# Two transformer layers on one core: another written order for the second layer's attention (jobs 60 ahead instead of 59)

## What is computed

```
x = x + attention_a(layernorm(x))      # 16 heads of 8, every query sees every key
x = x + ffn(layernorm(x))              # silu(x Wg) * (x Wu), then Wd; hidden 384
x = x + attention_b(layernorm(x))      # 16 heads of 8, causal: k_pos > q_pos is masked
x = x + ffn(layernorm(x))              # the same weights as the first ffn
```

## Time and profile before

| what | value |
|---|---|
| median of 3 runs | 1333.21 us (1331.5 to 1336.69) |
| the profiled execution | 1338.29 us, of which its span is 1336.4 us |
| PE busy | 1290.7 us, 97% of the span |
| DVE busy | 1176.7 us, 88% |
| ACT busy | 1004.5 us, 75% |
| first attention, full (from about 73 to 668 us) | 16 windows |
| causal attention, steady | from about 873 to 1222 us |

### The profile page before, as it was taken

One profiled execution on the slowest core, in us unless ns is written; L12 is line 12 of the kernel. 1 busy time (PEld: TensorE's weight loads), 2 busy tenths in 40 slices (PEclk: granted clock), 3 DMA queues, 4 the chain that ended last, 5 costly groups with the idle time before them and its releaser, 6 DMA issues.

```text
span 1336.4 us, 26857 instructions
## 1 busy us (share of the span) xinstructions
PE 1290.7 (97%) x9681; PEld 656.2 (49%) x9681; DVE 1176.7 (88%) x2979; ACT 1004.5 (75%) x1791; POOL 142.1 (11%) x309
## 2 busy tenths in 40 slices
PE   8899999999999999999988987999999999999998
PEld 6434343433434443434335764555555555555487
DVE  7699999999999999999926988799899999999276
ACT  8678888888888888888884531677777777777753
POOL 5630000000000000000002211200000000000011
PEclk9689999999999999999999996799999999999999
DMA  7611001111101111100000433112111211120001
GB/s 209 204 33 34 21 14 34 33 33 34 32 8 29 34 33 33 33 23 13 2 1 1 122 99 95 34 39 59 36 35 38 59 37 34 35 64 4 3 25 40
DMA packets 40060, 58.44 MB, mean 44 GB/s; under 512 B 7796, under 2 KB 19448, under 8 KB 39928
## 3 DMA queue, kind: packets, MB, share of 16 engines
q1 hardware_dynamic: 39928, 56.72, 17.7%
HBM read 36.77 MB, written 18.87 MB: 42 GB/s over the span
## 4 chain that ended last, share of the span: by engine, by line
PE 88%; DVE 5%; ACT 3%; issue 2%; DMA 1%; SPq 0%; POOL 0%; DVEq 0%; ACTq 0%; POOLq 0%
PE psum L1166 30%; PE psum L1132 21%; PE psum L1100 21%; PE psum L1253 4%; PE psum L1028 3%; PE psum L1237 2%; ACT probs L653 2%; PE psum L1140 2%; PE psum L1039 1%; DVE maxima L882 1%; DVE hid L958 1%; PE psum L1182 1%; PE psum L1077 1%; PE psum L1013 1%; PE psum L1150 1%
## 5 line engine op out<-in xcount | busy, mean ns | idle before, releaser
L653 ACT ACTIVATE probs<-psum 128x512 f32<-128x512 f32 (+3 forms) x1386 | 821.8, 669 | 153.0 <-PE psum L1132 83.0
L882 DVE TENSOR_REDUCE maxima<-psum 128x1 f32<-128x512 f32 x1232 | 767.8, 682 | 8.6 <-PE psum L1100 6.6
L1100 PE MATMUL psum<-kop,qop 62*128 62x512 f32 (+2 forms) x1744 | 519.4, 429 | 7.0 <-DVE maxima L879 3.1
L1132 PE MATMUL psum<-qop,kop 64*128 64x512 f32 (+3 forms) x1792 | 514.2, 427 | 9.2 <-ACT probs L653 7.9
L1166 PE MATMUL psum<-probs,v 128*32 128x512 f32 (+3 forms) x3584 | 440.5, 564 | 0.7 <-ACT sums L660 0.7
L1100 PEld LDWEIGHTS psum<-kop,qop 62*128 62x128 f32 x1744 | 266.4, 189 | 203.4 <-DVE maxima L882 119.3
L1132 PEld LDWEIGHTS psum<-qop,kop 64*128 64x128 f32 x1792 | 247.5, 187 | 232.1 <-ACT probs L653 205.9
L879 DVE CUSTOM_DVE_ANT_0 junk<-psum,mask 128x512 bf16<-128x512 f32 (+3 forms) x512 | 232.6, 487 | 38.7 <-PE psum L1100 34.9
L1166 PEld LDWEIGHTS psum<-probs,v 128*32 128x32 f32 x3584 | 71.1, 108 | 120.0 <-issue 89.2
L546 POOL TENSOR_TENSOR att<-att_raw,rden 128x128 f32<-128x128 f32 x64 | 26.1, 409 | 536.9 <-DVE rden L911 536.9
L1140 PE MATMUL psum<-half_ident,key_mask 64*128 64x64 bf16 x1024 | 74.3, 197 | 0.0
(11 more groups left out here) (102 smaller groups left out, 750.4 us busy)
## 6 DMA issues: line engine op xcount, KB each, us to landing
qop<-q_parts SPq DMA_DIRECT2D x256, 64.0 KB
kop<-k_parts SPq DMA_DIRECT2D x64, 128.0 KB
kop<-k_parts SPq DMA_DIRECT2D x128, 64.0 KB
q_parts<-parts SPq DMA_DIRECT2D x24, 256.0 KB, 2.9
k_parts<-parts SPq DMA_DIRECT2D x24, 256.0 KB, 3.2
x<-in_L_attn_a_x SPq DMA_DIRECT2D x8, 256.0 KB, 4.6
q_parts<-att SPq DMA_DIRECT2D x8, 256.0 KB, 3.7
k_parts<-att SPq DMA_DIRECT2D x8, 256.0 KB, 3.8
```

The source lines that it names most:

```text
L653: nc.scalar.activation(probs[:, slot, heads[0] % 2:heads[-1] % 2 + 1, c0:], psum[:, bank:bank + len(heads), c0:], ACT.Exp, scale=SCORE_SCA ...
L882: nc.vector.tensor_reduce(dst, src, AX_X, ALU.max).then_inc(ring_free, 1)
L1100: mm(psum[:, bank, 0:width], qop[rows, buf, f, r, qb * P:(qb + 1) * P].bitcast(F32R), kop[rows, buf, r, kh * CHUNK:kh * CHUNK + width].bit ...
L1132: ins = mm(psum[:, bank + k, c0:], kop[rows, buf, c // 2, j * P:(j + 1) * P].bitcast(F32R), qop[rows, buf, f, c // 2, c0:].bitcast(F32R), ...
```

## The change

One plan, that of the causal layer, gets another string, one more job ahead, and another order of the jobs within each half. Before, the turn of a window begins with two jobs, H, a job, a unit; the last sum of the window before (the first p) comes after three units (of steps 0, 0 and 1), and h, n, N stand together in the last quarter. After, the turn begins with two jobs and the owed sum, then H; n comes after two units and eight jobs of the new turn, and h and N stand together between the units of steps 6 and 7, without n. The numbers of letters are the same: 48 j, 24 s, 12 p and one each of H, h, N, n. `sums_behind` stays 1 and `project_at` stays (4, 6, 10).

```diff
          Plan(causal=True, heads=PAIR_UNITS, unit_ring=2, job_ring=3, alternate=True,
-              order="jjHjsjjsjjjspjssjjpjsjjsjspjjssjjpsjjpjssjjpjsjjsjpsjjjspjjssjjpjjsjspjjjhnNjjsjpjjssjjp",
-              jobs_ahead=59, sums_behind=1, project_at=(4, 6, 10),
-              tiles=("120 110 030 130 020 320 330 100 230 010 220 300 000 310 210 200",
...
+              order="jjpHjjsjjsjjnjjsjspjsjjspsjjspjsjsjjpsjjsjpsjjspjjhNjsjsjpjjssjjpjjsjsjjpjjssjjpjjsjsjp",
+              jobs_ahead=60, sums_behind=1, project_at=(4, 6, 10),
+              tiles=("200 010 230 330 000 130 320 020 100 030 110 120 310 210 300 220",
...
```

More of the change, by code:

```diff
@@ L156 @@
          Plan(causal=True, heads=PAIR_UNITS, unit_ring=2, job_ring=3, alternate=True,
-              order="jjHjsjjsjjjspjssjjpjsjjsjspjjssjjpsjjpjssjjpjsjjsjpsjjjspjjssjjpjjsjspjjjhnNjjsjpjjssjjp",
-              jobs_ahead=59, sums_behind=1, project_at=(4, 6, 10),
-              tiles=("120 110 030 130 020 320 330 100 230 010 220 300 000 310 210 200",
-                     "310 121 311 100 030 300 211 200 321 031 201 230 110 231 120 210 221 330 021 001 320 010 301 331 111 000 101 011 131 220 130 020"))]
+              order="jjpHjjsjjsjjnjjsjspjsjjspsjjspjsjsjjpsjjsjpjsjjspjjhNjsjsjpjjssjjpjjsjsjjpjjssjjpjjsjsjp",
+              jobs_ahead=60, sums_behind=1, project_at=(4, 6, 10),
+              tiles=("200 010 230 330 000 130 320 020 100 030 110 120 310 210 300 220",
+                     "301 030 311 021 031 320 011 101 000 310 330 231 201 110 100 210 010 131 111 130 220 121 020 120 230 331 221 211 300 200 321 001"))]
 SHIFT_PAIR = 2 * -(-[item[0] for item in PLANS[0].walk].index("shift") // 4)
```

## The result

The changed kernel took 1337.82 us (median of 20 runs, 1335.23 to 1342.44), the kernel before, run beside it, 1333.6 us (20 runs, 1331.5 to 1338.96). The ratio is 1.0026, with a 95% interval of 1.0015 to 1.0036: the change costs about 3.5 us. I had forecast 3.4 us gained.

A forecast was written before the change was run, and what follows sets the result against it. PE was taken as the bound, DVE close behind, ACT with room. Terms -3.2 - 0.5 + 0.3 = -3.4 us on 1333.21 gave 1329.8, forecast 1330; own range 1326 to 1332.5, 8-in-10 range 1322.5 to 1338.

The forecast's parts named there:

- ACT hides as before; cost 0, at worst 0.1 a period: Units of steps 4 to 8: PE has about 2.1 us for two units, ACT 75% busy, so no cost.
- The owed sum before H: Around H: two narrow sums let DVE catch up; PE's wait 0.58 becomes 0.35 us, 3.2 us gained over 14 periods.
- Rival 1: All waits go: none of the 0.58 us left, long periods normal, 9.1 gained, 0.3 lost, 1324.4 us; chance 0.18.
- n taken out of the bundle: Bundle h, n, N: no cost, at worst 0.2 us a period; three long periods shorten, 0.5 us gained, bounds 0 and 1.0.
- The end: Last turn, no jobs, ACT leads: n and N move ahead of the projection's start; 0, bounds 0.5 us either way.
- The start: Before window 0's first unit, 64 jobs instead of 62: net +0.3 us; clock unchanged, bounds 1.5 us either way.
- The sum: Whole kernel: -3.2 - 0.5 + 0.3 = -3.4 us, from the median 1333.21 to 1329.8, forecast as 1330.
- Rival 3: DVE becomes the bound in the nine jobs behind H: +0.6 a period, 1341.9 us, slower; chance 0.13.
- rival 4: Nothing moves: the wait changes its place and keeps its size, 1333.5 us; chance 0.14.
- Rival 2: Array's halves: fewer wide same-half neighbours on PE, 0.17 us each, 1.2 us a period, 1313 us; chance 0.03.
- ACT on the chain in steps 4 to 8: Sign in a steady window's chain of waits: seeing it would mean something the prediction had priced at nothing.

The follow-up runs named there:

- e5: Kernel before, DVE reducing only the last 128 columns of each causal-layer job, exponentials' scale times 0.001: 1323.93 us, period 26.48.
- e10: Changed kernel, ACT exponentiating only the first head of each causal-layer unit, DVE's jobs whole: 1328.77 us, period 26.60.
- e17: Changed kernel, ACT exponentiating only the first head of each unit in causal-layer steps 4 to 8: 1334.81 us, period 26.62.
- e12: Kernel before, heads 0 and 1, and 2 and 3, exchanged in every job (other array half): 1332.65 us, ratio 0.9989, period 26.73.
- e11: Changed kernel, heads 0 and 1, and 2 and 3, exchanged in every job (other array half): 1335.99 us, ratio 1.0011, period 26.94.
- e7: Kernel before, causal layer with 128-column DVE reductions and only each unit's first head exponentiated, exponentials' scale times 0.001: 1315.73 us, period 26.12.
- e6: Changed kernel, DVE reducing only the last 128 columns of each causal-layer job, exponentials' scale times 0.001: 1333.15 us, period 26.83.
- e1: Changed kernel's new string with the old order of jobs (`tiles`): 1370.31 us, ratio 1.0266 to the kernel before, period 28.93.
- e3: Changed kernel with n put back between h and N: 1344.83 us, ratio 1.008 to the kernel before, period 27.34.
- e13: Changed kernel, h and N moved to just ahead of step 9's units, one of five jobs around step 7 moved along: 1343.90 us, period 27.52.
- e15: Changed kernel, h and N moved to ahead of step 9, all five jobs staying around step 7: 1346.87 us, period 27.67.
- e18: Kernel before, ACT exponentiating only the first head of each unit in causal-layer steps 4 to 8: 1334.92 us, period 26.63.
- e4: Kernel before, n alone taken out of the bundle to ahead of the sum of step 0: 1349.55 us, ratio 1.0124, period 27.82.
- e14: Changed kernel, h and N moved to ahead of step 10, one of five jobs around step 7 moved along: 1352.45 us, period 28.07.
- e2: Kernel before, old string with the new order of jobs (`tiles`): 1367.56 us, ratio 1.0247, period 28.65.

## Why the prediction was wrong

**The step that failed** is "ACT hides as before; cost 0, at worst 0.1 a period". It cost 0.22 to 0.26 (e5 to e10), and 0.25 by the relief of steps 4 to 8 alone (0.36 in new, 0.11 in old). I had taken 2.1 us of PE's work between the units of a step against ACT's share of 75% over a whole window. A share over a window says nothing here: two wide units cost ACT 1.94 to 1.98 us, and at step 5 the copy of the sums (0.5) stands with them, about 2.45 us of ACT's time between the sums of steps 3 and 4, where PE without waits needs 1.79 (e17). ACT is the bound from step 4 to step 6, and idle in the narrow steps. Both lists have this stretch. Before, too, six exponentials follow without a gap (ACT's timeline of the kernel before), and relief in steps 4 to 8 gives old 0.11:

```profile
1014.98 0.60 ACT L660 COPY sums<-psum 128x512 f32<-128x512 f32 x1
1015.51 5.96 ACT L653 ACTIVATE probs<-psum 128x1024 f32<-128x1024 f32 x6
```

The new list loses more in it, 0.36 against 0.11. That the period's difference goes away with this relief is shown; that it is the pattern of the letters ("unit, jobs, unit, sum") rather than the widths of the jobs between them, or h and N beside step 7, was not tried apart.

**The owed sum before H.** I predicted 0.23 a period saved on waits for DVE. They went down by 0.07 to 0.11 (0.26 to 0.15 with ACT whole), with DVE off the chain. The sign was right and the size at most half. The 0.58 us on the chain, from which I started, was never worth 0.58: with DVE relieved (e5) the old period fell by 0.26 only, since other work of PE moved into its place. Rival 1 (14 x 0.58) had no such room either. (The nine jobs behind H add up to 3.89 us at the prices given, not 3.87, which changes nothing.)

**n taken out of the bundle.** No cost predicted, 0.15 measured in the transposes, and what is left with DVE and ACT relieved rose by 0.09 in all. The reciprocals were not shown to be the cause of the three long periods; in them DVE starts an instruction late, with nothing that it waited for (below), and there are six of them now. From windows 2 to 15 the means differ by 0.28, 0.04 more than the normal periods, so about 0.5 us in the kernel lost where I counted 0.5 gained.

**The end.** I took 0, bounds 0.5. The maxima are a bad mark for it, because the new list takes them earlier in a turn: from them to the next window's first exponential it is 25.28 us before (1006.77 to 1032.05) and 26.46 now (1000.40 to 1026.86). So the mark is that exponential. The last window's, and the last reciprocal, before and then now (ACT and DVE):

```profile
1244.51 1.94 ACT L653 ACTIVATE probs<-psum 128x1024 f32<-128x1024 f32 x2 [0.32 <-PE psum L1140]
1272.66 0.25 DVE L911 RECIPROCAL rden<-att_raw 128x16 f32<-128x16 f32 x1 [4.57 <-ACT att_raw L674]
```

```profile
1242.22 1.92 ACT L653 ACTIVATE probs<-psum 128x1024 f32<-128x1024 f32 x2
1270.53 0.26 DVE L911 RECIPROCAL rden<-att_raw 128x16 f32<-128x16 f32 x1 [4.56 <-ACT att_raw L674]
```

The last window takes 28.15 us before and 28.31 now, 0.16 more; with the halves exchanged it is the same pair (28.16 in e12, 28.32 in e11). With ACT relieved it is 25.90 in the old list and 25.15 in the new one, alike in e7 to e10. So ACT leads the end, and the term was inside its bounds.

**The start.** I had +0.3, bounds 1.5. It can't be read here: the second period is 29.47 us in this profile and 32.25 in that of before, and of kernels with the old list it was 29.27 in e12 and 28.5 in e5, with the new list 31.84 in e6. It goes with how long the clock stays at 0.50: until 842.8 us now, 854.2 before, 844.1 in e12, 839.0 in e5 and 846.9 in e6.

**The sum.** From the first exponential of window 1 (871.33 before, 864.84 now) to that of window 15, 14 periods at the clock of 1.00, it is 373.18 us before and 377.38 now: 4.2 more, and with the last window 4.4. Measured are 3.5 to 4.2. The rest of -0.2 to -0.9 would have to lie in the start; it is inside the bounds that I gave it, and not shown.

**The rivals.** None named ACT. Rival 3 had the right side for the wrong reason: DVE's waits fell. Against the measured change of +3.5 us, rival 4 (no change) lay nearest; against the median of 1337.82, rivals 3 (1341.9) and 4 (1333.5) are equally far. Rival 2 has the least for it, by e11 and e12 and by the six pairs on one half that became one without a gain. The place of the cause stood at the end of the prediction, as a sign to look for: "ACT on the chain in steps 4 to 8". Even that sign did not show, since the new kernel's chain reads all PE; ACT's waits there came out only when ACT was relieved. The range, 1322.5 to 1338, just held the median.

## What to carry to other kernels

Weigh an engine's room stage by stage, with all that stands on it there (here two exponentials and a copy, 2.45 us against 1.79), not by its share over a window. A chain that is all on one engine hides waits shorter than the overlap of its records; look for starts that follow another engine's end by a constant 0.05 us. Measure a stretch between marks that the change does not move. To find which of three coupled engines makes a difference, shorten the work of each in both kernels, and then in one stretch alone; moving one item of a tuned list changes too much at once.

## What the runs showed of the hardware

DVE starts an instruction late now and then, by some 0.35 us. Two cases of before (the idle time in front ends in "issue": DVE waited for nothing that the profile shows), and one of the new kernel:

```profile
1137.41 0.69 DVE L879 CUSTOM_DVE_ANT_0 junk<-psum,mask 128x512 bf16<-128x512 f32 x1 [0.28 <-issue]
...
1166.32 0.29 DVE L879 CUSTOM_DVE_ANT_0 junk<-psum,mask 128x128 bf16<-128x128 f32 x1 [0.28 <-issue]
```

```profile
1132.76 0.29 DVE L879 CUSTOM_DVE_ANT_0 junk<-psum,mask 128x128 bf16<-128x128 f32 x1 [0.43 <-PE psum L1100]
```

It goes by the count of instructions and not by time. With all of DVE's records in the trace counted from 0, those that only wait included, the late ones of windows 10 to 12 are numbers 2879, 3007 and 3135 in before, in new and in e1, e3, e5 to e13 and e15 to e18: 128 apart each time, of which 92 do work. In time this is 28.9 us before, 29.2 to 29.3 in new, 27.9 in e7 and 31.4 to 31.7 in e1. Number 2623, 256 earlier, starts late in most of them, too. In e4 and e14 only the last two of the three are late, in e2 none. A window of both lists has 116 such records, 84 of them with work, so the late start stands 12 records further on in each next window. A period is long (by 0.2 to 0.36) in windows 10 to 12 before and 8 to 13 after. In window 8 number 2623 is late in both (1048.89 and 1044.03), yet only the new period is longer; so it counts where DVE, or the PE that waits for its bank, has no slack. For windows 9 and 13 this was not followed. Why every 128th instruction is late is open.

Two matmuls on the two halves of the array start together, and two on the same half one after the other (0.16 to 0.28 us by width), yet six such neighbours a turn instead of one cost nothing that the period shows.
